# Residual sums between two scan layers: sixteen pieces on VectorE, six of them kept outside the image, and the normalisation cut to the piece that the next scan needs

## What is computed

```python
def _gn(v, G=16, eps=1e-05):              # over 3 channels and all pixels of one image
    ...
    return ((g - m) / jnp.sqrt(s + eps)).reshape(v.shape)

def _L1_conv_ref(x, down_w, down_b, ...): # _L2_conv_ref is the same with other weights
    # four scans, one after the other; each line depends on the line before it:
    #   line[i] = x[i] + conv1d(line[i-1], w, b)    K = 5, 48 -> 48 channels
    # down the rows, up the rows (same weights), then right and left over the columns
    ...

x = x + _L0_conv_ref(_gn(x), ...)   # 1x1 conv, 3x3 depthwise conv, channel attention, 1x1 conv
x = x + _L1_conv_ref(_gn(x), ...)   # scan layer 0
x = x + _L2_conv_ref(_gn(x), ...)   # scan layer 1
x = x + _L3_conv_ref(_gn(x), ...)   # gated MLP
```

## Time and profile before

| | us |
|---|---|
| median of 3 runs | 2779.28 |
| lowest and highest run | 2776.76, 2783.27 |
| the profiled execution, its own time | 2788.44 |
| its span, first to last instruction | 2786.6 |
| attention layer, up to the last matmul of its output convolution | about 928 |
| first gap, last convolution matmul to first scan matmul | about 17 |
| scan layer 0 | about 687 |
| second gap | about 109 |
| scan layer 1 | about 684 |
| last gap and MLP | about 362 |

### The profile page before, as it was taken

The page is one execution under the profiler, slowest core; times in us unless marked ns, Lnnn a source line. Parts: engine busy times, 40 slices in busy tenths (PEclk is TensorE's granted clock), DMA queues, the critical chain, the costliest instruction groups (busy, mean ns, idle before and its releaser), DMA issues.

```text
span 2786.6 us, 45599 instructions
## 1 busy us (share of the span) xinstructions
PE 2432.4 (87%) x18588; PEld 2128.5 (76%) x18588; DVE 1349.0 (48%) x3238; ACT 753.1 (27%) x1167; POOL 205.8 (7%) x257
## 2 busy tenths in 40 slices
PE   1999999999999799999999940999999999737595
PEld 1999948948942599999999940999999999713343
DVE  3323354354355444444555575444445555567465
ACT  3524354354357100441005523002430000012121
POOL 1000000000000460000000035000000000000311
PEclk9999999999999899999999975999999999958897
DMA  8740000004002400000000048200000000195434
GB/s 149 145 85 5 1 1 1 1 1 91 1 1 46 91 1 1 1 1 1 1 1 1 1 107 227 40 1 1 1 1 1 1 1 1 41 270 182 131 99 128
DMA packets 75558, 129.88 MB, mean 47 GB/s; under 512 B 10224, under 2 KB 59600, under 8 KB 70448
## 3 DMA queue, kind: packets, MB, share of 16 engines
q1 hardware_dynamic: 68064, 123.36, 19.1%
q10 hardware_dynamic: 7184, 3.84, 0.5%
q0 software_dynamic: 128, 0.01, 0.0%
HBM read 76.85 MB, written 50.33 MB: 46 GB/s over the span
## 4 chain that ended last, share of the span: by engine, by line
PE 78%; DVE 7%; DMA 6%; ACT 4%; issue 2%; SPq 1%; POOL 1%; ACTq 0%; POOLq 0%; DVEq 0%
PE bank L965 17%; PE bank L966 16%; PE bank L967 16%; PE bank L868 14%; PE bank L930 6%; PE bank L883 3%; PE bank L873 3%; ACT work L642 3%; DMA work<-saved 2%; PE bank L1069 2%; DVE stats L1093 1%; DMA image<-flat_rows 1%; DMA work<-in_x 1%; DMA saved<-image 1%; SPq L334 1%
## 5 line engine op out<-in xcount | busy, mean ns | idle before, releaser
L1286 DVE TENSOR_TENSOR image<-bank,image 112x128 f32<-112x128 f32 x2032 | 660.4, 325 | 712.4 <-PE bank L967 712.4
L965 PE MATMUL bank<-image,scan_wt 112*112 112x128 f32 x4064 | 809.0, 280 | 37.9 <-ACT image L716 31.2
L966 PE MATMUL bank<-image,scan_wt 112*112 112x126 f32 x4064 | 771.9, 271 | 0.0
L967 PE MATMUL bank<-image,scan_wt 112*112 112x126 f32 x4064 | 770.4, 270 | 0.0
L965 PEld LDWEIGHTS bank<-image,scan_wt 112*112 112x112 f32 x4064 | 567.3, 175 | 42.6 <-ACT image L716 31.4
L966 PEld LDWEIGHTS bank<-image,scan_wt 112*112 112x112 f32 x4064 | 581.6, 176 | 0.0
L967 PEld LDWEIGHTS bank<-image,scan_wt 112*112 112x112 f32 x4064 | 579.1, 176 | 0.0
L868 PE MATMUL bank<-work 112*128 112x192 f32 x2304 | 423.3, 332 | 10.5 <-issue 10.5
L642 ACT ACTIVATE work<-image,gn_shift,gn_scale 48x567 f32<-48x567 f32 (+5 forms) x384 | 334.6, 904 | 315.6 <-PE bank L873 220.4
L868 PEld LDWEIGHTS bank<-work 112*128 112x128 f32 x2304 | 374.3, 193 | 12.9 <-issue 12.4
L734 ACT COPY work<-image 48x256 f32 x192 | 80.5, 419 | 730.3 <-PE bank L967 729.9
(11 more groups left out here) (148 smaller groups left out, 1525.2 us busy)
## 6 DMA issues: line engine op xcount, KB each, us to landing
work<-saved SPq DMA_DIRECT2D x64, 384.0 KB, 11.7
image<-flat_rows SPq DMA_DIRECT2D x4, 3072.0 KB, 14.3
out<-image SPq DMA_DIRECT2D x8, 1536.0 KB, 6.9
saved<-image SPq DMA_DIRECT2D x12, 768.0 KB, 9.8
saved<-image SPq DMA_DIRECT2D x6, 1536.0 KB, 17.6
flat_rows<-image SPq DMA_DIRECT2D x46, 192.0 KB, 5.3
band<-in_x SPq DMA_DIRECT2D x16, 384.0 KB, 5.6
work<-in_x SPq DMA_DIRECT2D x16, 384.0 KB, 5.7
```

What stands on the lines that cost most here:

```text
L965: mm(dst, wt[:, 1], src, start=True, stop=False)
L966: mm(dst[:, 1:J2, :], wt[:, 0], src[:, 0:J2 - 1, :], start=False, stop=False)
L967: mm(dst[:, 0:J2 - 1, :], wt[:, 2], src[:, 1:J2, :], start=False, stop=True).then_inc(s_prod[g], 1)
L1286: v.tensor_tensor(line(g, along_w, at), prod, line(g, along_w, src), ALU.add).then_inc(s_state[g], 1)
```

## The change

It has five parts.

1. The unit of both gaps is a piece of 2048 columns: 16 rows of both images of a pair (both parities, 1024 columns each). A pair has 8 pieces, numbered t = 0 to 15 over the two pairs. In HBM a piece is two runs of 1024 columns for each partition.
2. Before the first scan only piece 0 of each pair is normalised (ACT for pair 0, DVE for pair 1). ACT does the others while scan 0 runs, and PE and DVE wait for `s_ready` at every sixteenth row of it. Exception: in the second gap all of pair 0 is done ahead. `s_tail` is gone, and so are the four pieces of L716 between the blocks of the last image.
3. The raw save of pair 1 in the first gap has one semaphore for each of its four parts (`s_raw`), and a piece waits for its own part only.
4. In the second gap DVE makes all 16 sums, each followed by its four statistics instructions. GpSimd makes none. There are 6 buffers, loaded ahead. The last 6 sums (t = 10 to 15) are written to the buffers and not to `image`, and are saved from there (`s_late`), while ACT normalises from the buffer to `image`.
5. SP saves each piece by itself after its sum, behind the fetch of piece t + 6. Two later things wait for `s_late` and `s_ready`: SP before it fetches the residual of the last gap, and GpSimd before it builds its constants.

```diff
-VCH = 2
-V_COLS = 5120
+GAP = 6
+HELD = 2 * (K2 // 8) - GAP
...
-        back = kept[0:PER]
+        back = kept + [cut(at - 256 - CHUNK, [CHUNK], P)]
...
+        def unsaved(eng, layer, t):
+            if layer == 0:
+                eng.wait_ge(*((s_save, 32) if t < NBLK else (s_raw[t % NBLK // 2], 32)))
+            elif t < HELD:
+                eng.wait_ge(s_keep[t // NBLK], 32 * (NBLK, HELD - NBLK)[t // NBLK])
...
+            for t in range(GAP):
+                bring(t)
+            for t in range(2 * NBLK):
+                sp.wait_ge(s_kept_v, t + 1)
+                if t < HELD:
+                    bring(t + GAP)
+                save(t, s_keep[t // NBLK] if t < HELD else s_late)
+            sp.wait_ge(s_keep[0], 32 * NBLK)
+            sp.wait_ge(s_keep[1], 32 * (HELD - NBLK))
+            sp.wait_ge(s_late, 32 * GAP)
+            sp.wait_ge(s_ready, 2 * (NBLK - 1))
...
-                    pool.wait_ge(s_back[m], b * 32 + 32)
-                    dst = image[0:P, ds(b * IMG + m * CHUNK, CHUNK)]
-                    nc.gpsimd.tensor_tensor(dst, dst, back[m], ALU.add).then_inc(s_kept_p, 1)
...
+                normalise(layer, 0).then_inc(s_state[0], 1)
+                for n in range(1, NBLK if layer else 1):
+                    normalise(layer, n)
                 deviation(2 * layer + 3, 2, NB)
...
+                for n in range(1, NBLK):
+                    if layer == 0:
+                        normalise(layer, n)
+                    normalise(layer, NBLK + n).then_inc(s_ready, 1)
...
+                if scan == 0 and at and at % 16 == 0:
+                    pe.wait_ge(s_ready, layer * (NBLK - 1) + at // 16)
...
+                    for t in range(2 * NBLK):
+                        dve.wait_ge(s_back[t % GAP], 32 * (t // GAP + 1))
+                        dst = piece(image if t < HELD else back[t % GAP], t)
+                        v.tensor_tensor(dst, piece(image, t), piece(back[t % GAP], t), ALU.add).then_inc(s_kept_v, 1)
+                        last = sums(t)
```

More of the change, by code:

```diff
@@ L255, in build @@
         s_x1 = sem("s_x1")
-        s_save = [sem(f"s_save{g}") for g in range(2)]
+        s_save = sem("s_save")
+        s_raw = [sem(f"s_raw{i}") for i in range(SAVES)]
         s_keep = [sem(f"s_keep{g}") for g in range(2)]
@@ L262, in build @@
         s_swap = sem("s_swap")
-        s_tail = sem("s_tail")
-        s_back = [sem(f"s_back{i}") for i in range(PER)]
+        s_ready = sem("s_ready")
+        s_late = sem("s_late")
+        s_back = [sem(f"s_back{i}") for i in range(GAP)]
         s_kept_v = sem("s_kept_v")
-        s_kept_p = sem("s_kept_p")
         s_x2 = [sem(f"s_x2_{i}") for i in range(KEPT)]
@@ L395, in _ @@
             for half, rows in enumerate((LO, HI)):
-                sp.dma_start(saved[0][half, :, 0:2 * IMG], image[rows, 0:2 * IMG]).then_inc(s_save[0], 16)
+                sp.dma_start(saved[0][half, :, 0:2 * IMG], image[rows, 0:2 * IMG]).then_inc(s_save, 16)
             for i in range(SAVES):
@@ L428, in _, with bring @@
-            sp.wait_ge(s_kept_v, NB * VCH)
-            save_columns(NB - 1, 0, VCH * CHUNK)
-            sp.wait_ge(s_kept_p, NB * (PER - VCH))
-            save_columns(NB - 1, VCH * CHUNK, IMG)
-            sp.wait_ge(s_keep[0], 64)
-            sp.wait_ge(s_keep[1], 96)
+                    sp.dma_start(dst, src).then_inc(s_raw[i], 16)
+            sp.wait_ge(s_save, 32)
+            for i in range(SAVES):
+                sp.wait_ge(s_raw[i], 32)
+            sp.wait_ge(s_back_gap, GAP)
+            def bring(t):
+                g, n = t // NBLK, t % NBLK
+                for half, rows in enumerate((LO, HI)):
+                    src = saved[0][half].rearrange("c (g s n) -> c g s n", g=2, s=2)
+                    sp.dma_start(piece(back[t % GAP], t)[rows],
+                                 src[:, g, :, n * 2 * BN:(n + 1) * 2 * BN]).then_inc(s_back[t % GAP], 16)
@@ new lines, in save @@
+            def save(t, signal):
+                g, n = t // NBLK, t % NBLK
+                for half, rows in enumerate((LO, HI)):
+                    dst = saved[1][half].rearrange("c (g s n) -> c g s n", g=2, s=2)
+                    sp.dma_start(dst[:, g, :, n * 2 * BN:(n + 1) * 2 * BN],
+                                 piece(image if t < HELD else back[t % GAP], t)[rows]).then_inc(signal, 16)
+            for t in range(GAP):
[5 more added lines that the diff above has]
+                save(t, s_keep[t // NBLK] if t < HELD else s_late)
@@ L552, in _ @@
                 pool.wait_ge(s_state[g], PASSES * STEPS + 1)
-            with pool.Fori(0, NB) as b:
-                for m in range(VCH, PER):
-                    pool.wait_ge(s_back[m], b * 32 + 32)
-                    dst = image[0:P, ds(b * IMG + m * CHUNK, CHUNK)]
-                    nc.gpsimd.tensor_tensor(dst, dst, back[m], ALU.add).then_inc(s_kept_p, 1)
+            pool.wait_ge(s_late, 32 * GAP)
+            pool.wait_ge(s_ready, 2 * (NBLK - 1))
             ms(w1_sb, 0.0)
@@ L709, in _, with normalise @@
             attention(NB - 2, True)
-            def normalise(layer, b, c0, c1):
-                act.wait_ge(s_gn, 2 * layer + 3 + b // 2)
-                act.wait_ge((s_save, s_keep)[layer][b // 2], RAW_SAVED[layer][b // 2])
-                v = image_n[:, b // 2, b % 2, c0:c1]
-                return nc.scalar.activation(v, v, ACT.Identity, bias=gn_shift[0:P, b:b + 1],
-                                            scale=gn_scale[0:P, b:b + 1])
+            def normalise(layer, t):
+                act.wait_ge(s_gn, 2 * layer + 3 + t // NBLK)
+                unsaved(act, layer, t)
+                src = summed(t) if layer else piece(image, t).rearrange("p s (n b) -> p b s n", b=2)
+                dst = piece(image, t).rearrange("p s (n b) -> p b s n", b=2)
+                for i in range(2):
+                    b = t // NBLK * 2 + i
+                    last = nc.scalar.activation(dst[:, i], src[:, i], ACT.Identity, bias=gn_shift[0:P, b:b + 1],
+                                                scale=gn_scale[0:P, b:b + 1])
+                return last
             for n in range(NBLK):
@@ L1282, in step @@
                 src = (at - 1) % H if ahead else at
+                if scan == 0 and at % 16 == 0:
+                    dve.wait_ge(s_ready, layer * (NBLK - 1) + at // 16)
                 for g in range(2):
```

75 lines of the change are left out of this document (22 added, 53 removed).

## The result

The changed kernel takes 2757.09 us (median of 3 runs, 2754.92 to 2759.33) against 2779.28 us: ratio 0.9912, 95% interval 0.9884 to 0.9939. Run again beside more runs of the kernel before it gave 0.9908 (0.9895 to 0.9921), a gain of 25.6 us. So it is faster, and inside the range, but the forecast of 36 us was some 11 us too much, and the time itself lies 14 us over the 2743 that was forecast.

A forecast was written before the change was run, and what follows sets the result against it. PE's work and the gaps in it were taken to bound the kernel. First gap 14.6 us plus second gap 22.4 gave 37.0, less 1 us: 36 off the median 2779.3, so 2743 us, range 2739 to 2759.

The forecast's parts named there:

- (a): Ahead of the first gap: no large pieces on ACT between the last image's blocks, gain 2.0 us.
- (b): First gap: DVE's wait for the save of pair 1 goes, gain 5.7 us.
- (c): First gap: DVE normalises 2 x 1024 columns instead of 2 x 5120, 1.2 us; ACT's 6.7 us leave the path.
- the rival at 2747: Scan 0: ACT's added work slows the steps by 5% for 57 us, costing 3 us; chance 0.04.
- I take 1 us off: Whole kernel: 1 us of the gain deducted for 28 added waits and a clock that may rise a little later.
- (d): Second gap: sixteen sums on DVE at 2.29 us, each with four statistics instructions at 2.42 us, 75.4 us.
- (e): Second gap: two group norms at 4.4 us each, 8.8 us.
- (f): Second gap: the last normalisation, 1.2 us.
- Do the transfers keep up?: Second gap: at 275 GB/s, 5.7 us for a fetch and a save, the last fetch is in time by 8 us or more.
- unmixed rates: Second gap: fetches 4.9 us and saves 3.6 us a piece, last fetch 9.8 us late, kernel 2753 us; chance 0.15.
- a price for each transfer: Second gap: each transfer costs 2.4 us whatever its bytes, last sum 18.9 us late, kernel 2762 us; chance 0.07.
- The price for each packet: Second gap: saves cost 0.72 us a packet, last sum 54.8 us late, kernel 2798 us; chance 0.06.

The follow-up runs named there:

- the filled kernels: Matmuls on unused columns while PE waits: added to the changed kernel, 2743.94 and 2742.19 us; added to the kernel before, 90 in each gap, 2790.93 us.
- the second profile: Kernel before, unchanged, run against itself with another profile: 2782.98 against 2783.07 us, ratio 1.0001; its second gap took 102.6 us.

## Why the prediction was right, and where it was off

**What bounds the kernel; first gap.** Right. (a) was forecast at 2.0 us; blocks 2 to 6 take 35.82 us and not 37.97, 2.15 less, and the whole stretch to the final statistics was 1.5 to 2.3 us shorter in the profiles with this part. (b) and (c) were forecast at 12.6 us and gave 12.2: there is no wait for a save, but the two instructions of 1024 columns take 1.54 us where scaling from 5120 columns had given 1.2. With (a) the change gave 13.7 us of the 14.6; the start came 15.3 us earlier in this profile because the convolutions ahead happened to be 1.6 us faster.

**The work pushed into scan 0.** Priced at zero, and ACT's pieces did not make PE or DVE wait: one took 1.21 us, under the 1.35 assumed. That ACT's traffic slows the steps (the rival at 2747) did not show: with the clock equal, the layer is 0.9 us longer, in seven steps of 0.12 us at the added waits.

**"I assume that PE starts as cold as before" and "I take 1 us off".** This is a term that was mis-sized. PE has pair 0's first row and an idle 1.5 us behind it before pair 1 starts, and its clock came up 6.4 us after that start, where it had come up after 2.1; in layer 1 it was 5.2 where it had been 2.2. Half speed over 4.3 and 3.0 more us costs 2.1 and 1.5 us, and the filled kernels show 1.7 and 1.2. With the added waits, 0.9 and 0.7, the scans give back 4.5 us, where 1 us had been allowed for both together.

**Second gap.** Forecast 22.4 us, and from the profile that it was worked from it gave 107.8 - 85.8 = 22.0. (d): a sum and its statistics follow the last ones after 4.71 us (1621.58 to 1626.29), 75.4 us for sixteen, as forecast. (e): 4.39 us for each group norm (the second from 1701.42 to 1705.81), 8.8 us, as forecast. (f): 1.5 us for 1.2.

**Do the transfers keep up?** Right, and with more room than was claimed. Fetches and saves in runs of 4 KB ran at 296 GB/s, 5.3 us for a fetch and a save. So DVE waited for no fetch: the last one was issued by 1672.1, and with 6.5 us to landing an estimate for its arrival is 1679, some 18 us before its sum at 1696.6. The rivals fall with it: unmixed rates (8.5 us for the two), and a price for each transfer, since 36 transfers of 384 KB went in 48 us, 1.33 us each and not 2.4. With 6.5 to 7.0 us from issue to landing, about five of them were under way at a time. The price for each packet falls too: 48 us x 16 engines x 0.977 / 4046 packets are 0.19 us each, and not 0.55 or more. The Trainium skill's advice of at least 1 MiB for a transfer ("DMA: Bandwidth & Descriptors", Bandwidth), named in the prediction as speaking against the change, shows no loss here where it isn't followed: the transfers of 384 KB ran at 296 GB/s, and the mix of them with saves of 1536 KB in the kernel before at 275. ACT could begin on pair 0 at 1667.7, 46.1 us after the first sum, where 49 (1683.3) had been the earlier estimate.

**The sum.** This is the term that was off most. The prediction took the gain off the median of the runs as if the 9.2 us by which the profiled execution stood above it lay somewhere else. They did not: 5.2 us of the difference to an execution near the median are the waits for transfers and for GpSimd in the second gap, and the change removes those waits, however long they are. A change that removes a scattering wait gains its typical length, and 16.8 us is what it gains against the second profile. (That this profile's gap is the typical one rests on it and on one of 104.4 us, both of executions near their medians.) So 36 us less 5.2 for the waits and 3.5 for the scans (4.5 where 1 had been allowed) is 27 us, against 25.6 measured with an interval of 22 to 29 us. The rest of the 14 us between 2757 and 2743 is the median of before: 2779.28 in three runs, 2783.07 in nineteen on another chip.

**The range.** The 2757 lies inside 2739 to 2759 by luck. The upper end was put there for the unmixed rates, which did not come, and for a worthless (a), which gave 1.5 to 2.3 us. What filled the room instead were the scattering waits and the clock, for which the range had 3 us of scatter and 1 us.

**What stays open.** Why the transfers of the kernel before take 3 to 5 us more in some executions, why the last part varies between 356 and 366 us, and why the fillers gain more between some medians (13 us) than in the stretches (9 us).

## What to carry to other kernels

Before you subtract a gain from a median, see whether the profiled execution's excess lies in the very wait that you remove; a second profile of the same kernel tells. A gap that gets shorter is not only time won: look at the clock in the first microseconds behind it, and at whether PE has something to do in it, since filler matmuls in the waits took 9 us off the scans and the second gap here for a few lines. And of a bundle of edits, try each alone: holding sums in buffers was the most elaborate part of this one, and gave nothing.

## What the runs showed of the hardware

- Filler matmuls of 128 columns, 38 for the first layer and 51 for the second, held the granted clock at 1.00 at the starts of both, where it was 0.83 (920 to 950 us) and 0.58 (1700 to 1715 us), and took 9 us off the two scan layers and the gap between them.
- A busy GpSimd slows VectorE unevenly. With products of 512 columns beside them, sums of 2048 columns took 2.86 us for 2.28; statistics took the same 0.68; four of the two-column operations took 0.9 to 1.0 us for 0.16 to 0.23.
- In runs of 4 KB, one save for each fetch gave 296 GB/s, and two gave 253 with the queue less busy. Fetches alone gave some 160. So the even mix was the fastest of the three; saves alone in such runs were not seen.
- A wait that is already met is not free with PE saturated: each sixteenth row of the scan, with one such wait on PE and one on DVE, came 0.12 us later.
